# Projections from f16 parts, and row maxima combined between the turns of the next iteration

## Chip, cores and metric

One core of a Trainium2 chip. The time is that of the whole kernel on the device, in microseconds; the median of three runs before the change is 1688.91 (1688.57 to 1694.19).

## What is computed

A pre-norm block over x of shape (4, 2048, 256): causal attention with 16 heads of 16, then a product with int8-rounded operands.

```python
x = x + attn(layernorm(x), Wq, Wk, Wv, Wo, bo)
#   q, k, v = x @ Wq, x @ Wk, x @ Wv, split in 16 heads of 16
#   weights = softmax(q k^T / 4, causal); out = (weights v) @ Wo + bo
x = x + ffn(layernorm(x), rhs)
#   rows of the left operand and columns of rhs are scaled by their absolute maximum / 127,
#   rounded to integers, multiplied, scaled back
```

## The kernel before

There are two blocks of code. `project` goes over 16 chunks of 512 tokens. A chunk is normalised (statistics on VectorE, from chunk 2 on the normalisation itself on GpSimd, L595), transposed on TensorE in f32 (L773), copied to `xnT` by ScalarE (L732), and multiplied with the three weights in f32: four blocks of q and k (L792, j = 0 to 3, two products of 512 columns each), then two groups of v (L803, eight products of 256 columns each). The transposes of chunk n + 1 stand between q, k and v of chunk n. ScalarE casts each q or k block to f16 (L743), VectorE takes the rest as a second f16 part (L650), and both parts go to HBM. GpSimd also fills constants in K and V at the start.

`attend` goes over 16 iterations (4 batches by 4 groups of 4 heads). An iteration has 36 steps (`STEPS`, from the last query chunk to the first), each of two pairs of heads: TensorE makes scores (L1025), ScalarE takes exp (L1214), GpSimd masks the diagonal steps (L1277), TensorE multiplies with V three steps later (L1044). The scores need the row maximum subtracted, and that is inside the product: the negated maxima stand as two f16 rows in Q. They are found one iteration ahead by 68 "turns": TensorE makes a pair of banks of scores (`max_turn_on_pe`, L261 off the diagonal, L275 and L280 on it), VectorE reduces them (`max_turn_on_dve`, L353). Two pairs of banks alternate, so turn n needs turn n - 2 taken (`mx_free`). The 69th turn of an iteration is the tail: `combine_maxima` on VectorE (L308 to L316) makes negm and its two f16 parts, TensorE transposes them (L291), VectorE copies them to mT (`take_maxima`, L326), and SP writes four row transfers to Q (`max_rows`, L224), for which the scores of the next iteration's first step wait.

Every engine's queue is in the order of the program. On TensorE the order in `attend` is a table by hand, `BEFORE`: for each of the 72 pairs of an iteration how many turns come ahead of the value blocks, how many value blocks, how many turns behind them; then come the pair's scores. In pairs 58 to 62 it reads (2, 0, 0), (0, 2, 0), (0, 2, 0), (0, 1, 1), (2, 0, 0): two turns, then four value blocks with no turn, a fifth, the tail, and two turns of the next iteration. The turns of the first iteration are spread over chunks 2 to 13 of the projections, six places a chunk, behind each j and about v; its tail is in chunk 14, and the first 12 turns of the next iteration are in chunks 14 and 15. A last phase (output projection, second normalisation, integer product) runs under the last iteration and behind it.

## Time and profile before

| | us |
|---|---|
| median of the runs | 1688.91 |
| span of the profiled execution | 1686.8 |
| around the span (the difference of these) | 2.1 |
| attention block begins on TensorE | 249.6 |
| last turn's reduce ends, all engines | about 1455 |
| TensorE busy | 1603.7 |
| VectorE busy | 1516.0 |
| ScalarE busy | 1330.8 |
| GpSimd busy | 290.6 |

The busy time of TensorE counts the modelled drain of each matmul, so a busy TensorE isn't one without gaps. A group's mean is the length of one instruction with its start and drain; instructions of one engine overlap by some 0.07 to 0.2 us, so the pace is read from starts. "Idle before" is time of an engine just before an instruction, with what ended it; "issue" means nothing that the profile shows.

### The profile page before, as it was taken

What the parts mean: (1) busy time and instruction counts of PE and PEld (TensorE: products, weight loads), DVE (VectorE), ACT (ScalarE), POOL (GpSimd) and SP (SyncE); (2) the same over time, 40 slices, a digit from 0 to 9 for tenths busy, and PEclk for the clock granted to TensorE, in tenths of its full rate; (3) what the DMA queues carried; (4) which work ended last, traced back from release to release, by engine and by line L of the source; (5) the groups of instructions that cost most, each with busy time, mean ns of one, the idle gap of its engine ahead of it and who ended that gap; (6) DMA issues with size and microseconds to landing.
All of it is one profiled execution on the core that took longest, in us unless ns stands there. A gap on an engine that the chain in (4) does not pass through costs nothing.

```text
span 1686.8 us, 39739 instructions
## 1 busy us (share of the span) xinstructions
PE 1603.7 (95%) x16319; PEld 643.5 (38%) x16319; DVE 1516.0 (90%) x1812; ACT 1330.8 (79%) x2610; POOL 290.6 (17%) x363
## 2 busy tenths in 40 slices
PE   6999999999999999999999999999999999999965
PEld 3445443333333333333333333333333333344433
DVE  4677779999999999999999999999999999678876
ACT  2233338999999999999999999999999999877651
POOL 5333310201020202111111111111112020100120
PEclk9999999999999999999999999999999999999986
DMA  3443320111121212121212112121212143034532
GB/s 108 146 136 117 112 89 12 39 34 40 33 77 37 74 38 68 43 62 43 62 47 59 54 52 59 46 60 46 59 46 67 47 115 88 14 105 136 159 116 70
DMA packets 105609, 118.73 MB, mean 70 GB/s; under 512 B 20688, under 2 KB 87508, under 8 KB 105428
## 3 DMA queue, kind: packets, MB, share of 16 engines
q1 hardware_dynamic: 105428, 116.19, 23.8%
q8 instruction: 129, 2.11, 0.5%
...
## 4 chain that ended last, share of the span: by engine, by line
DVE 54%; PE 27%; issue 1%; ACT 1%; DMA 1%; SPq 1%; POOL 0%; ACTq 0%; DVEq 0%
DVE pmax L353 46%; PE psum L1044 11%; PE psum L1025 6%; DVE pblk L353 4%; PE psum L1084 3%; PE psum L261 3%; PE psum L280 2%; PE psum L275 2%; DMA f_rs<-inverse_sums 1%; DVE V L1323 1%; ACT prob L1214 1%; PE psum L1108 1%; DVE V L1342 1%; DVE V L1330 1%; DVE f_amax L1348 1%
## 5 line engine op out<-in xcount | busy, mean ns | idle before, releaser
L1214 ACT ACTIVATE prob<-psum 128x512 f32<-128x512 f32 (+1 forms) x2304 | 1181.0, 574 | 136.7 <-PE psum L1025 113.2
L353 DVE TENSOR_REDUCE pmax<-psum 128x2 f32<-128x1024 f32 (+1 forms) x960 | 1101.0, 1216 | 13.5 <-PE psum L280 6.5
L1044 PE MATMUL psum<-prob,V 128*32 128x256 f32 x8704 | 676.0, 391 | 0.0
L1025 PE MATMUL psum<-Q,K 50*128 50x512 f16 (+3 forms) x2560 | 464.7, 349 | 3.8 <-ACT prob L1214 1.0
L1277 POOL TENSOR_SCALAR_AFFINE_SELECT prob<-prob 128x512 f32<-128x512 f32 x256 | 160.6, 640 | 1185.3 <-ACT prob L1214 1182.8
L261 PE MATMUL psum<-K,Q 48*128 48x512 f16 x1536 | 298.4, 385 | 13.5 <-DVE pmax L353 13.5
L1044 PEld LDWEIGHTS psum<-prob,V 128*32 128x32 f32 x8704 | 181.5, 108 | 294.2 <-issue 214.1
L1025 PEld LDWEIGHTS psum<-Q,K 50*128 50x128 f16 x2560 | 174.6, 94 | 251.3 <-ACT prob L1214 185.1
L261 PEld LDWEIGHTS psum<-K,Q 48*128 48x128 f16 x1536 | 74.3, 93 | 272.0 <-DVE pmax L353 212.8
L353 DVE TENSOR_REDUCE pblk<-psum 128x8 f32<-128x1024 f32 x128 | 151.8, 1219 | 5.8 <-PE psum L280 5.6
L280 PE MATMUL psum<-K,Q 48*128 48x512 f16 (+3 forms) x1024 | 128.6, 298 | 0.0
L275 PE MATMUL psum<-mask,maskid 64*128 64x128 bf16 (+2 forms) x1280 | 103.6, 230 | 9.3 <-DVE pmax L353 5.3
L743 ACT CAST part<-psum 128x512 f16<-128x512 f32 x64 | 37.5, 586 | 91.8 <-PE psum L792 91.8
L650 DVE TENSOR_TENSOR part<-psum,part 128x512 f16<-128x512 f32 x64 | 44.3, 692 | 60.5 <-ACT part L743 60.5
L595 POOL TENSOR_SCALAR f_x<-f_x,mv,rstd 128x256 f32<-128x256 f32 x56 | 67.7, 1223 | 117.2 <-DVE rstd L635 116.9
L275 PEld LDWEIGHTS psum<-mask,maskid 64*128 64x128 bf16 x1280 | 58.4, 95 | 62.9 <-DVE pmax L353 35.1
L1084 PE MATMUL psum<-f_wo,f_us 128*128 128x256 f32 x256 | 76.5, 429 | 0.0
L803 PE MATMUL psum<-wv,xnT 128*128 128x256 f32 x256 | 63.1, 390 | 0.0
L792 PE MATMUL psum<-xnT,wq 128*128 128x512 f32 x128 | 62.0, 617 | 1.1 <-DVE wq L688 1.1
L792 PE MATMUL psum<-xnT,wk 128*128 128x512 f32 x128 | 62.5, 614 | 0.0
L753 ACT COPY V<-psum 128x512 f32<-128x512 f32 x32 | 18.8, 586 | 46.1 <-PE psum L803 46.1
L1084 PEld LDWEIGHTS psum<-f_wo,f_us 128*128 128x128 f32 x256 | 47.5, 204 | 18.0 <-issue 12.6
...
## 6 DMA issues: line engine op xcount, KB each, us to landing
...
Q<-q_parts SPq DMA_DIRECT2D x128, 64.0 KB, 2.5
K<-k_parts SPq DMA_DIRECT2D x128, 64.0 KB, 2.1
...
```

The source lines that it names most:

```text
L261: return nc.tensor.matmul(bank, Q[p][rows, pair, qt * P:(qt + 1) * P], K[p][rows, pair, kc * CH:(kc + 1) * CH], start=True, stop=True)
L275: nc.tensor.matmul(to, maskid[at:at + HALF, i, :], mk, start=i == 0, stop=False, skip_group_check=True)
L280: m = nc.tensor.matmul(bank[:, col:col + n], Q[p][rows, pair, qt * P:(qt + 1) * P], K[p][rows, pair, a * CH:a * CH + n], start=False, stop ...
L353: nc.vector.tensor_reduce(to, of, axis=AX.X, op=ALU.max).then_inc(M.mx_free, 1)
L595: i = nc.gpsimd.tensor_scalar(xn[s][:, t, :], xs[s][:, t, :], mv[s][:, t, 0:1], rstd[s][:, t:t + 1], ALU.subtract, ALU.mult)
L792: m = nc.tensor.matmul(PS[:, j, :], w[i][:, k, o * P:(o + 1) * P], xnT[s][:, k, :], start=k == 0, stop=k == KC - 1)
L803: m = nc.tensor.matmul(PS[:, 2 + j, (t % 2) * D:(t % 2 + 1) * D], xnT[s][:, k, t * P:(t + 1) * P], w[2][:, k, :], start=k == 0, stop=k == ...
L1025: m = nc.tensor.matmul(PS[:, SB + i % RING, at:at + n], K[it % 2][rows, pair, kb * P:(kb + 1) * P], Q[it % 2][rows, pair, (c + 1) * CH - n ...
L1044: m = nc.tensor.matmul(PS[32 * h:32 * h + 32, UB, to:to + n], V[:, it // NG * NT + kb, col:col + 32], prob[(it * NSTEP + k) % PRING][:, h, ...
L1084: m = nc.tensor.matmul(bank[:, q % 2 * D:(q % 2 + 1) * D], us[j % 4][:, o, q * P:(q + 1) * P], wo[:, o, :], start=False, stop=o == KC - 1, ...
L1214: nc.scalar.activation(prob[g % PRING][:, h, 0:n], PS[:, SB + i % RING, 0:n], ACT.Exp, scale=by).then_inc(exp_done, 1)
L1277: nc.gpsimd.affine_select(out=d, in_=d, compare_op=ALU.is_ge, fill=0.0, base=0, pattern=[[0, G], [1, P]], channel_multiplier=-1).then_inc( ...
```

## The change

The parts of the projection: x and the weights are each split into two f16 parts, high and low, and three of the four products of parts are added in PSUM (`TERMS`), so a f32 product becomes three f16 ones. The q and k weights are scaled by a power of two and split on VectorE; the v weight is transposed, scaled by powers of two for each output column, split, and transposed back, and Wo is scaled by the inverse in `attend` on GpSimd (two operations of 128x256 in iteration 1). x is normalised in halves, ScalarE casts each half (`high_rows`), GpSimd subtracts (`low_rows`), TensorE transposes both parts in f16, ScalarE copies both. `root(1)` now stands ahead of `take_xT(0)`.

The parts of the maxima: pmax and pblk exist twice, by the parity of the iteration. The tail of iteration it - 1 is no longer right behind its last turn but between the fifth and the sixth turn of iteration it (`BETWEEN`). VectorE does the blocks behind the first of these turns and negm behind the second; GpSimd does the split into parts; ScalarE copies the transposed parts to mT. A tail gives nothing to `mx_free`; the turn two behind it waits for `mT_ready`. The first iteration's tail stays whole in chunk 14, and the last one's is at the end. `BEFORE` and `AHEAD` are as they were.

```diff
...
+TERMS = ((0, 0), (1, 0), (0, 1))
...
-    turns, tail = [], []
+    turns, tail, last = [], [], []
     for it in range(ITS):
-        turns += [(it, kind) for kind in (KINDS if it else sorted(KINDS, key=lambda kind: max(chunks_of(kind))))]
-        tail.append(len(turns))
-        turns.append((it, None))
-    return turns, tail
-
-
-TURNS, TAIL = order_of_turns()
+        kinds = KINDS if it else sorted(KINDS, key=lambda kind: max(chunks_of(kind)))
+        for i, kind in enumerate(kinds):
+            if it >= 2 and i == BETWEEN:
+                tail.append(len(turns))
+                turns.append((it - 1, None))
+            turns.append((it, kind))
+        last.append(len(turns) - 1)
+        if it in (0, ITS - 1):
+            tail.append(len(turns))
+            turns.append((it, None))
+    return turns, tail, last
+
+
+BETWEEN = 5
+TURNS, TAIL, LAST = order_of_turns()
+
+
+def handed_back(n):
+    return sum(kind is not None or it == 0 for it, kind in TURNS[:n])
 
...
+def pairs_of_turns():
+
+    out, turn = {}, BEGUN
+    for it in range(ITS):
+        for pair in range(2 * NSTEP):
+            back = turns_until(it, pair)[1]
+            for n in range(turn, back):
+                out[n] = (it, pair)
+            turn = max(turn, back)
+    return out
+
+
+PAIR_OF = pairs_of_turns()
+TAKEN_AT = {PAIR_OF[TAIL[it]]: it for it in range(1, ITS)}
+PARTS_AT = {PAIR_OF[min(LAST[it] + 2, TAIL[it])]: it for it in range(1, ITS)}
...
-        pe.wait_ge(mx_free, n - 1)
+        pe.wait_ge(mx_free, handed_back(n - 1))
+        if TURNS[n - 2][1] is None and TURNS[n - 2][0] >= 1:
+            pe.wait_ge(M.mT_ready, TURNS[n - 2][0] + 1)
     at = MB + 2 * (n % 2)
...
+def blocks_to_maxima(nc, dve, it, M):
+
+    dve.wait_ge(M.mx_free, handed_back(LAST[it] + 1))
+    blk = M.pblk[it % 2][:].rearrange("p f h a j -> p (f h a) j")
+    top = M.pmax[it % 2][:].rearrange("p f h (a t) j -> p (f h a) t j", t=TPC)
     nc.vector.tensor_reduce(top[:, :, 2, 3], blk[:, :, 0:3], axis=AX.X, op=ALU.max)
-    nc.vector.tensor_copy(top[:, :, 0, 3], blk[:, :, 3]).then_inc(comb, 1)
-    dve.wait_ge(comb, it * COMB + 1)
-    nc.vector.tensor_reduce(negm[:], pmax[:].rearrange("p f h q j -> p (f h q) j"), axis=AX.X, op=ALU.max,
-                            negate=True).then_inc(comb, 1)
-    dve.wait_ge(comb, it * COMB + 2)
-    nc.vector.tensor_scalar(mparts[:, 0, :], negm[:], 1.0 / ONE, None, ALU.mult).then_inc(comb, 1)
-    dve.wait_ge(comb, it * COMB + 3)
+    nc.vector.tensor_copy(top[:, :, 0, 3], blk[:, :, 3]).then_inc(M.blocks_in, 1)
+
+
+def negated_maxima(nc, dve, it, M):
+
+    dve.wait_ge(M.blocks_in, it + 1)
+    if it >= 1:
+        dve.wait_ge(M.mp_ready, it)
+    nc.vector.tensor_reduce(M.negm[:], M.pmax[it % 2][:].rearrange("p f h q j -> p (f h q) j"), axis=AX.X, op=ALU.max,
+                            negate=True).then_inc(M.negm_ready, 1)
+
+
+def split_maxima(nc, dve, M):
+
+    negm, mparts = M.negm, M.mparts
+    dve.wait_ge(M.negm_ready, 1)
+    nc.vector.tensor_scalar(mparts[:, 0, :], negm[:], 1.0 / ONE, None, ALU.mult).then_inc(M.first_part, 1)
+    dve.wait_ge(M.first_part, 1)
     nc.vector.scalar_tensor_tensor(out=mparts[:, 1, :], in0=negm[:], scalar=1.0 / ONE, in1=mparts[:, 0, :],
                                    op0=ALU.mult, op1=ALU.subtract).then_inc(M.mp_ready, 1)
 
 
+def split_maxima_on_pool(nc, pool, it, M):
+
+    negm, mparts, scaled = M.negm, M.mparts, M.scaled
+    pool.wait_ge(M.negm_ready, it + 1)
+    pool.wait_ge(M.mT_ready, it)
+    nc.gpsimd.tensor_scalar(scaled[:], negm[:], 1.0 / ONE, 1.0, ALU.mult, ALU.mult).then_inc(M.first_part, 1)
+    pool.wait_ge(M.first_part, 3 * it - 1)
+    nc.gpsimd.tensor_copy(mparts[:, 0, :], scaled[:]).then_inc(M.first_part, 1)
+    pool.wait_ge(M.first_part, 3 * it)
+    nc.gpsimd.tensor_tensor(mparts[:, 1, :], scaled[:], mparts[:, 0, :], ALU.subtract).then_inc(M.first_part, 1)
+    pool.wait_ge(M.first_part, 3 * it + 1)
+    pool.sem_inc(M.mp_ready, 1)
+
...
+def take_maxima_on_act(nc, act, it, PS, M):
+
+    n = TAIL[it]
+    act.wait_ge(M.mrows_in, it * M.MROWS)
+    act.wait_ge(M.mx_ready, n + 1)
+    nc.scalar.copy(M.mT[:], PS[:, M.MB + 2 * (n % 2), :].bitcast(F16)[:, 0:P]).then_inc(M.mT_ready, 1)
+
+
...
-                pool.wait_ge(xn_ready, n)
-                pool.wait_ge(tposed, n - 1)
+                pool.wait_ge(xn_ready, 2 * n)
+                pool.wait_ge(xl_ready, 2 * n - 2)
                 for t in range(TPC):
-                    i = nc.gpsimd.tensor_scalar(xn[s][:, t, :], xs[s][:, t, :], mv[s][:, t, 0:1],
-                                                rstd[s][:, t:t + 1], ALU.subtract, ALU.mult)
-                i.then_inc(xn_ready, 1)
-
-
-            pool.wait_ge(w_scaled, 2)
-            pool.wait_ge(xn_ready, 2)
+                    i = nc.gpsimd.tensor_scalar(xn[s][:, t, :], xs[s][:, t, :], nmean[s][:, t:t + 1],
+                                                rstd[s][:, t:t + 1], ALU.add, ALU.mult)
+                    if t % 2 == 1:
+                        i.then_inc(xn_ready, 1)
+
+            def low_rows(n):
+                s = n % 2
+                for half in range(2):
+                    at = slice(2 * half, 2 * half + 2)
+                    pool.wait_ge(xh_ready, 2 * n + half + 1)
+                    if n >= 2 and half == 0:
+                        pool.wait_ge(tposed, n - 1)
+                    nc.gpsimd.tensor_tensor(xp[s][:, 1, at, :], xn[s][:, at, :], xp[s][:, 0, at, :],
+                                            ALU.subtract).then_inc(xl_ready, 1)
+
...
+            low_rows(2)
...
+            def scale_value_weight():
+
...
+                dve.wait_ge(vT_raw, 1)
+                of = PS[:, 6, :].rearrange("p (o r) -> p o r", o=KC)
+                nc.vector.tensor_reduce(cmax[:], of, axis=AX.X, op=ALU.max,
...
+                dve.wait_ge(v_step, 5)
+                for o in range(KC):
+                    nc.vector.tensor_scalar(vT[:, 0, o, :], of[:, o, :], cinv[:, o:o + 1], None,
+                                            ALU.mult).then_inc(v_step, 1)
+                dve.wait_ge(v_step, 5 + KC)
+                for o in range(KC):
+                    i = nc.vector.scalar_tensor_tensor(out=vT[:, 1, o, :], in0=of[:, o, :], scalar=cinv[:, o:o + 1],
+                                                       in1=vT[:, 0, o, :], op0=ALU.mult, op1=ALU.subtract)
+                i.then_inc(vT_split, 1)
 
             statistics(0)
             variance(0)
-            nc.vector.memset(M.pmax[:], NEG).then_inc(pmax_set, 1)
+            for s in range(2):
...
+            def high_rows(n, half):
+                s, at = n % 2, slice(2 * half, 2 * half + 2)
+                act.wait_ge(xn_ready, 2 * n + half + 1)
+                if n >= 2 and half == 0:
+                    act.wait_ge(tposed, n - 1)
+                nc.scalar.copy(xp[s][:, 0, at, :], xn[s][:, at, :]).then_inc(xh_ready, 1)
+
             def take_xT(n):
                 act.wait_ge(tposed, n + 1)
                 if n >= 2:
                     act.wait_ge(v_ready, (n - 1) * KC)
-                nc.scalar.copy(xnT[n % 2][:], PS[:, 0:2, :]).then_inc(xT_ready, 1)
+                for i in range(2):
+                    nc.scalar.copy(xT[n % 2][:, i].rearrange("p k t -> p (k t)"),
+                                   PS[:, i, :].bitcast(F16)).then_inc(xT_ready, 1)
 
             root(0)
+            for half in range(2):
+                high_rows(0, half)
+            root(1)
             take_xT(0)
-            root(1)
+            for half in range(2):
+                high_rows(1, half)
+            act.wait_ge(vT_back, 1)
+            nc.scalar.copy(wp[2][:].rearrange("p i k c -> p (i k c)"),
+                           PS[:, 7, :].bitcast(F16)).then_inc(wv_ready, 1)
             for n in range(NC):
                 s = n % 2
                 for j in range(QK):
                     if n >= 2 and j == 0:
                         act.wait_ge(stored[s], n // 2 * STORES)
                     nc.scalar.copy(part[s][0][:, j], PS[:, j, :]).then_inc(hi_ready, 1)
+                    if j % 2 == 1 and 2 <= n + 1 < NC:
+                        high_rows(n + 1, j // 2)
                 if n + 1 < NC:
                     take_xT(n + 1)
...
             def transpose(n):
                 s = n % 2
-                pe.wait_ge(xn_ready, n + 1)
+                pe.wait_ge(xl_ready, 2 * n + 2)
                 if n >= 1:
                     pe.wait_ge(lo_ready, (n - 1) * QK + 2)
-                for f in range(KC):
-                    for t in range(TPC):
-                        i = nc.tensor.transpose(PS[:, f, t * P:(t + 1) * P], xn[s][:, t, f * P:(f + 1) * P],
-                                                identf[:])
-                i.then_inc(tposed, 1)
-
-            transpose(0)
+                for i in range(2):
+                    for f in range(KC):
+                        for t in range(TPC):
+                            at = (f * TPC + t) * P
...
+                        for o in range(KC):
+                            at = ((i * KC + k) * KC + o) * P
+                            m = nc.tensor.transpose(PS[:, 7, :].bitcast(F16)[:, at:at + P],
+                                                    vT[:, i, o, k * P:(k + 1) * P], identh[:])
+                m.then_inc(vT_back, 1)
+
             pe.wait_ge(wmax_ready, 1)
             nc.tensor.transpose(PS[0:2, 7, 0:P], wmax[:], identf[:]).then_inc(wmaxT, 1)
+            value_weight(False)
+            transpose(0)
...
             nc.tensor.matmul(PS[:, 7, 256:258], ones2[:], gdiag[:], start=True, stop=True).then_inc(pow_spread, 1)
             for n in range(NC):
                 s = n % 2
-                pe.wait_ge(xT_ready, n + 1)
+                pe.wait_ge(xT_ready, 2 * n + 1)
...
-                        pe.wait_ge(w_scaled, i + 1)
+                        pe.wait_ge(w_scaled, 2 * i + 2)
                     if n >= 1 and i == 1:
                         pe.wait_ge(v_taken, (n - 1) * KC + o + 1)
-                    for k in range(KC):
-                        m = nc.tensor.matmul(PS[:, j, :], w[i][:, k, o * P:(o + 1) * P], xnT[s][:, k, :],
-                                             start=k == 0, stop=k == KC - 1)
+                    for of_w, of_x in TERMS:
+                        if j == 0 and of_x == 1:
+                            pe.wait_ge(xT_ready, 2 * n + 2)
+                        for k in range(KC):
+                            m = nc.tensor.matmul(PS[:, j, :], wp[i][:, of_w, k, o * P:(o + 1) * P],
+                                                 xT[s][:, of_x, k, :], start=(of_w, of_x, k) == (0, 0, 0),
+                                                 stop=(of_x, k) == (1, KC - 1))
                     m.then_inc(qk_ready, 1)
+                    if n == 0 and j == 1:
+                        value_weight(True)
                     turns(n, j)
...
                             act.wait_ge(p_free, g - PRING + 1)
                         nc.scalar.activation(prob[g % PRING][:, h, 0:n], PS[:, SB + i % RING, 0:n],
                                              ACT.Exp, scale=by).then_inc(exp_done, 1)
+                        if h % 2 == 1 and (it, 2 * k + h // 2) in TAKEN_AT:
+                            take_maxima_on_act(nc, act, TAKEN_AT[it, 2 * k + h // 2], PS, M)
                         if h % 2 == 1 and it + 1 == ITS:
                             for p, u in units_at(2 * k + h // 2):
                                 unit(p, u)
...
                     if k == ENDS[1] + 1 and 2 <= it < WHOLE + 2:
                         normalise_group(it - 2)
+                    for pair in (2 * k, 2 * k + 1):
+                        if (it, pair) in PARTS_AT:
+                            split_maxima_on_pool(nc, pool, PARTS_AT[it, pair], M)
...
-                if it >= 2 and n == (TAIL[it] + TAIL[it - 1]) // 2:
+                if it >= 2 and n == (LAST[it] + LAST[it - 1]) // 2:
                     invert(it - 2)
-                max_turn_on_dve(nc, dve, n, PS, M)
+                if TURNS[n][1] is not None:
+                    max_turn_on_dve(nc, dve, n, PS, M)
+                if it >= 2 and n == LAST[it - 1] + 1:
+                    blocks_to_maxima(nc, dve, it - 1, M)
+                if it >= 2 and n == LAST[it - 1] + 2:
+                    negated_maxima(nc, dve, it - 1, M)
+            blocks_to_maxima(nc, dve, ITS - 1, M)
+            negated_maxima(nc, dve, ITS - 1, M)
```

## Rows read from the trace of the kernel before

**Rows 1.** The page, part 4: chain that ended last, share of the span by line.
```profile
DVE pmax L353 46%; PE psum L1044 11%; PE psum L1025 6%; DVE pblk L353 4%; PE psum L1084 3%; PE psum L261 3%; PE psum L280 2%; PE psum L275 2%; DMA f_rs<-inverse_sums 1%; DVE V L1323 1%; ACT prob L1214 1%; PE psum L1108 1%; DVE V L1342 1%; DVE V L1330 1%; DVE f_amax L1348 1%
```
**Rows 2.** VectorE in order of time, iteration 4: start us, us, operation, count, idle before.
```profile
602.81 0.54 DVE L1289 RECIPROCAL f_inv<-f_sums 128x64 f32<-128x64 f32 x1
...
610.51 30.63 DVE L353 TENSOR_REDUCE pmax<-psum 128x2 f32<-128x1024 f32 x27
...
641.13 2.36 DVE L353 TENSOR_REDUCE pblk<-psum 128x8 f32<-128x1024 f32 x2
...
643.53 0.20 DVE L308 TENSOR_REDUCE pmax<-pblk 128x16 f32<-128x48 f32 x1
...
643.85 0.42 DVE L311 TENSOR_REDUCE negm<-pmax 128x64 f32<-128x256 f32 x1
...
645.47 0.23 DVE L326 COPY mT<-psum 128x128 f16<-128x128 f16 x1 [0.71 <-PE psum L291]
...
646.05 3.72 DVE L353 TENSOR_REDUCE pmax<-psum 128x2 f32<-128x1024 f32 x3 [0.35 <-PE psum L280]
...
683.91 0.54 DVE L1289 RECIPROCAL f_inv<-f_sums 128x64 f32<-128x64 f32 x1
```
**Rows 3.** TensorE (PE matmul, PEld weight load) in order of time, same place.
```profile
641.19 0.12 PEld L275 LDWEIGHTS psum<-mask,maskid 64*128 64x128 bf16 x4 [0.39 <-DVE pmax L353]
...
645.13 0.10 PEld L291 LDWEIGHTS psum<-identh,mparts 128*128 128x128 f16 x1 [0.41 <-issue]
...
645.39 0.26 PEld L275 LDWEIGHTS psum<-mask,maskid 64*128 64x128 bf16 x4
...
651.18 0.39 PE L261 MATMUL psum<-K,Q 48*128 48x512 f16 x2
```
**Rows 4.** Projection stage in order of time: first chunk, chunk 2, a steady chunk, chunk 14.
```profile
17.90 5.63 PE L792 MATMUL psum<-xnT,wq 128*128 128x512 f32 x8 [1.07 <-DVE wq L688]
...
19.50 0.38 DVE L630 BATCH_NORM_AGGREGATE mv<-stats 128x2 f32<-128x6 f32 x4
...
54.72 1.41 DVE L623 BATCH_NORM_STATS2 stats<-f_x 128x6 f32<-128x256 f32 x4 [2.79 <-DMA f_x<-in_L_attn_x]
...
59.64 1.88 PE L792 MATMUL psum<-xnT,wq 128*128 128x512 f32 x4
...
107.78 0.39 PE L261 MATMUL psum<-K,Q 48*128 48x512 f16 x2
...
108.10 1.98 PE L792 MATMUL psum<-xnT,wk 128*128 128x512 f32 x4
...
110.01 0.39 PE L261 MATMUL psum<-K,Q 48*128 48x512 f16 x2
...
116.48 1.99 PE L803 MATMUL psum<-wv,xnT 128*128 128x256 f32 x8
...
219.74 3.60 PE L792 MATMUL psum<-xnT,wq 128*128 128x512 f32 x8
```
**Rows 5.** A bf16 product of the last phase; two groups by line (busy, mean ns).
```profile
1507.79 1.05 PE L1108 MATMUL psum<-f_wq,V 128*128 128x256 bf16 x8
...
L743 ACT CAST part<-psum 128x512 f16<-128x512 f32 x64 | 37.5, 586 | 91.8 <-PE psum L792 91.8
...
L1247 POOL TENSOR_TENSOR f_rs<-f_rs 128x1024 f32<-128x1024 f32 x12 | 28.4, 2367 | 9.3 <-DMA f_rs<-inverse_sums 9.2
```
**Rows 6.** SP's transfers of the maxima, their landing, and the scores that need them.
```profile
645.78 2.50 SPq L224 DMA_DIRECT2D Q<-mT  x4
...
DMA to landing us min/median/max: 1.8/1.9/3.2
...
656.89 0.38 PE L1025 MATMUL psum<-Q,K 50*128 50x512 f16 x2
```
**Rows 7.** Windows: span, busy (count) by engine PE to POOL, PEclk, DMA share, GB/s.
```profile
54.50:57.50 3.00, 0.23 (x6) 0.19 (x7) 2.78 (x10) 0.59 (x1) 0.00 (x0) 1.00 0.54 185
...
254.00:258.00 4.00, 3.98 (x34) 1.86 (x30) 3.83 (x4) 2.65 (x7) 0.00 (x0) 0.50 0.01 4
```

141 lines of the change are left out of this document (99 added, 42 removed).

## The prediction

> **What bounds the kernel now.** I read the chain of waits by line first [rows 1]: VectorE's row-maximum reduces (pmax and pblk, L353) are half of it, the rest mostly TensorE. Then VectorE in order of time over one period of the attention stage [rows 2]. The same reciprocal comes at 602.81 and 683.91, so an iteration takes 81.10 us. Twenty-seven reduces take 30.63, thus (30.63 - 1.22) / 26 = 1.131 us each when they follow each other, and 68 of them are 76.9; the reciprocal is about 0.5; from the natural end of the second pblk (641.13 + 2 x 1.13 = 643.40) to the next turn (646.05) go 2.65. Sum 80.05; about 1.0 is small idle time. VectorE has no slack: what is taken from it or made idle counts one to one, unless TensorE can't follow. Then TensorE around that place [rows 3]: it issues the last turn of the iteration's maxima at 641.19 and reaches the transposition of the maxima at 645.13 without waiting for VectorE (its idle time there is "issue"). In between it does scores and five value blocks. So VectorE's combining sits beside 3.94 us in which TensorE has no turn to give it. That is what decides this part.
> The projection stage [rows 4] is different: from chunk 3 (59.64) to chunk 14 (219.74) a chunk takes 160.1 / 11 = 14.55 us, and TensorE's products follow each other. It is bound by TensorE there.
>
> **Projections, steady chunks.** Now: a q or k block of two f32 products is 110.01 - 108.10 = 1.91 us, its turn 108.10 - 107.78 = 0.32. No row shows f16 products of 128 rows and 512 columns; the nearest are eight bf16 ones of 256 columns in 1.05, 0.21 of it the drain, so about 0.107 each [rows 5]. Six of 512 columns are then 1.28, with the change of weights some 1.35: 0.55 saved, four times, 2.2 a chunk. A value group (eight f32, 1.99 with 0.2 of drain) becomes twelve of 0.107: 1.3, so 0.5 saved twice, 1.0. Transposes: f16, twice as many, taken as equal. TensorE thus saves 3.2. Against this there is a new chain before the transposes of the next chunk. The second `high_rows` stands on ScalarE behind the cast of j = 3, and the second `low_rows` on GpSimd behind that, while TensorE waits in order for xl_ready with V, the turns and the next chunk queued behind. After the last k product: cast 0.6 [rows 5], high part of 128x512 0.7 (a cast from SBUF, estimated a little over the cast from PSUM), low part 1.2 (half of GpSimd's 128x1024 two-input operation, 2.37) [rows 5], 0.1 of semaphores: 2.6; only the turn (0.32) covers it. Stall 2.3. Before, xn was long ready. The two xT copies (1.0 each instead of one) lie beside V, the normalisation on GpSimd lies before, and VectorE's work of about 11 a chunk stays under 13.4. Net 0.9 to 1.15 a chunk; I take 1.15, since the blocks of turns also shrink: 11 x 1.15 = 12.7. Bounds: if the low part took half or twice as long, the net is 1.75 or 0, so 19 or 0. Chunk 14 brings 0.9, and chunk 15, which has no next transposes, 2.1 before VectorE's eight turns bind.
> **Its start.** `root(1)` now stands ahead of `take_xT(0)`, so the first product, at 17.90 now, waits for a variance that ends at 19.88 now, and later still behind two more weight operations; then VectorE's split of the value weight and TensorE's transposes of it stand ahead of k of chunk 0, all of it behind ScalarE and GpSimd, whose 7 us fills of K follow. I estimate chunk 1 three us late, chunk 2 four. But at 54.72 VectorE idles 2.79 for x [rows 4], and a stall of the same kind stands before the chunk before; both vanish in the delay. Left at chunk 3: +1.3 (bounds 0 and +5).
> Projection stage: +1.3 - 12.7 - 0.9 - 2.1 = -14.4, bounds -24 and +3.
>
> **Combining, taken apart, iteration by iteration.** VectorE loses the two splits, the wait for TensorE's transposition (0.71 [rows 2]) and the copy to mT; it keeps blocks (643.53 to 643.85, 0.32) and negm (0.42). On paper 2.65 - 0.74 = 1.9 saved. But the table BEFORE, which places turns among scores and values, is unchanged: two value blocks, twice, and no turn between LAST and the 70th place. So the first turn of the next iteration takes the place of the old transposition, at 645.13. From the weight load of such a diagonal turn to VectorE's start go 646.05 - 645.39 = 0.66: it starts at 645.79, and VectorE idles from 643.40 until then, 2.4 us, because blocks_to_maxima is written behind that turn and not in the hole. Then: turn 645.79 to 646.92, blocks to 647.24, turn to 648.37, negm to 648.83, three turns to 652.2. The old end of the same five turns is 652.00. So far +0.2.
> TensorE must be checked along: the third turn needs the first one done (646.92; before, the short mT copy freed that bank at 645.7), so TensorE stands 1.2 longer there, with scores and values queued behind it, and runs about 1.1 late to the fifth turn; that is just in time for VectorE.
> Then comes the transposition, now between the fifth and the sixth turn, and it takes one of the two banks. TensorE may issue the sixth turn only when VectorE is through with the fifth, at 652.2, instead of at 651.18 ahead of need [rows 3]. A turn of this kind takes about 0.45 from issue to VectorE's start (0.39 of it the product): after the 0.2 for issuing, VectorE starts at 652.87 instead of 652.00. That makes +0.87, and another 0.15 follow, since TensorE, 1.2 late, has less lead for the two turns after it. An iteration thus gets 1.0 longer instead of 1.9 shorter. Bounds: if TensorE's values slid forward into the gaps, 0; if each of the bubbles is half as large again, +2.2; the paper value -1.9 is the far end. 14 iterations have this order (the tails of 1 to 14): 14 x 1.0 = +14, bounds -27 and +31.
> Beside it: the split on GpSimd is three operations of 64 columns; by 2.37 for 1024 columns 0.15 each, with starts and semaphores 0.7 to 1.2 in all. It starts at 648.9 and TensorE comes for it at about 651: hidden, with a second to spare, and the masking of the same step comes after it in time for values three steps later. The copy on ScalarE costs some 0.2 a period there, and ScalarE had idle time. It stands behind the exponentials of its pair of heads, so mT is ready at 653.3 and not at 645.7. SP then issues four transfers (2.50) and they land 1.9 after issue [rows 6]: about 657.2. The first scores that need them stood at 656.89; they are 1.0 later, 657.9. Hidden, by 0.7. What else SP has to store or load at that time waits for later steps anyway. The last tail has no turn behind it and frees nothing that anyone waits for: 0. Scaling Wo on GpSimd, the second copies of pmax and pblk: 0.
>
> **The sum.** The profiled execution has a span of 1686.8; the runs' median is 1688.91, 2.1 more for what lies around the span. 1686.8 - 14.4 + 14 = 1686.4; with 2.1, 1688.5.
>
> **Rivals.**
> (a) *The combining gain comes through.* TensorE's stretch at 641.19 to 645.13 would have to shrink, or VectorE to catch up elsewhere. For it: VectorE is the first line of the chain. Against it: the stretch in [rows 3] has no wait in it that could go. -27 - 14: 1688.9 - 41 = 1648. Chance 0.12; half-way cases 0.05.
> (b) *The chain behind the cast costs less* (GpSimd's low part at half the price, or the start hidden): projections -24, combining +14: 1679. With combining at +7: 1672. For it: the 1.2 is from f32 in and out. Chance 0.18.
> (c) *The row maxima come too late.* Place: scores of the next iteration, step 0. From 0.7 us more than I count (a landing took up to 3.2 [rows 6], against 1.9), TensorE stops there, and each us beyond, less the 0.4 of lead that VectorE has, lengthens 14 iterations. At 1.7 more: 14 x 0.9 = +13, so 1702, slower than before. Chance 0.15. Slower without this, by bubbles of twice the size or a dearer start: 1698 to 1710, chance 0.05.
> (d) *TensorE's clock falls in the new stalls.* It stood at 0.50 (1.2 GHz) in 254 to 258, after TensorE had worked little at the change of stages, but at 1.00 (2.4 GHz) through the wait of 54.5 to 57.5 [rows 7], which is longer than my 2.3. If it fell in each of 12 chunks for those 4 us, TensorE would lose 2 us of work each time: +24, 1713. Chance 0.07.
> The Trainium skill, "TensorE: Matmul & The Clock Gate", Part 4 (PE-mode transpose), says that transposes don't count as activity for the clock gate; by it, stall and transposes together, about 3.3 us, are one quiet stretch. The rows show no such stretch in this stage, so this stays the small chance just given.
> (e) Forecast as summed: 0.38, its own range 1680.5 to 1697.
>
> **How the numbers follow.** Within 0.5% (8.4 us, about what a measurement can tell from no change): (e), 0.38. Faster: (a) 0.17 and (b) 0.18, 0.35. Slower: (c) 0.20 and (d) 0.07, 0.27. Range for 8 in 10: from between (b) and (a), 1664, to between (c) and (d), 1710. The time is that of (e), 1688.5.
>
> **What would show it.** Right: VectorE idle 2.2 to 2.6 once an iteration ahead of the first diagonal turn, released by TensorE, then 0.5 ahead of the sixth turn; period near 82.1; chunks of 13.4 with 2.3 of TensorE waiting for GpSimd ahead of the transposes; attention beginning about 14 earlier than at 249.6. Wrong: a period under 81, or of 83 and more with TensorE waiting for a DMA at the first scores; chunks under 12.5 or over 14; a clock of 0.50 inside the projections.

## The result, and the profile after

| | before | after |
|---|---|---|
| median of the runs, us | 1689.88 (1688.57 to 1694.19, 4 runs) | 1705.09 (1700.72 to 1706.28, 4 runs) |
| span of the profiled execution | 1686.8 | 1704.5 |
| attention begins on TensorE | 249.62 | 250.04 |
| one iteration of attention | 81.10 | 81.92 |

The changed kernel takes 1.0079 of the time before (95% interval 1.0064 to 1.0094): slower by 13 us by this ratio (by 15 by the two medians), where I had forecast no change. The ledger of the two profiled executions, by VectorE's reciprocals, one an iteration: the first stands level (359.51 and 359.44); thirteen periods of +0.82 are 10.7 (1413.84 and 1424.47); the one behind them, with the last maxima, takes 75.03 instead of 73.50, +1.5; so 12.2 at the end of attention, and the 5.5 that are left of 17.7 arise in the last phase. There the additions of VectorE keep a distance of 12.16 to those of before for ten tiles (1476.97 and 1489.13 the first, 1577.36 and 1589.52 the tenth) and then drift off, in a stretch in which the granted clock was 0.84 before and 0.81 after. From the last of these reciprocals to the end it takes 199.5 before and 205.0 here, and between 199.5 and 204.5 in the other kernels of this document, whose edits leave that phase alone. So I count no step of the change for it.

The projection stage of after, against [rows 4]: the first products of q in chunks 0, 3 and 14, one turn of the stall, the x that VectorE waits for, and SP's load of it.
```profile
24.22 4.90 PE L959 MATMUL psum<-f_rs,wpq 128*128 128x512 f16 x12 [5.91 <-ACT f_rs L865]
...
69.68 1.46 PE L959 MATMUL psum<-f_rs,wpq 128*128 128x512 f16 x6
...
98.66 2.75 PE L959 MATMUL psum<-f_rs,wpq 128*128 128x512 f16 x12
...
107.38 1.07 PE L918 MATMUL psum<-identh,f_us 128*128 128x128 f16 x16 [2.01 <-POOL f_us L684]
...
221.04 2.75 PE L959 MATMUL psum<-f_rs,wpq 128*128 128x512 f16 x12
```
```profile
50.57 1.41 DVE L713 BATCH_NORM_STATS2 stats<-f_x 128x6 f32<-128x256 f32 x4 [6.67 <-DMA f_x<-in_L_attn_x]
...
63.82 1.41 DVE L713 BATCH_NORM_STATS2 stats<-f_x 128x6 f32<-128x256 f32 x4 [5.37 <-DMA f_x<-in_L_attn_x]
```
```profile
46.51 0.42 SPq L628 DMA_DIRECT2D f_x<-in_L_attn_x  x1
...
59.89 0.43 SPq L628 DMA_DIRECT2D f_x<-in_L_attn_x  x1
```
Against 17.90, 59.64 and 219.74 of before, chunk 0 starts 6.3 later, chunk 3 10.0 later and chunk 14 1.3 later. The stall for GpSimd is there, 2.01. The wait for x, 2.79 before, did not vanish in the delay: it has grown to 5.37, and the one a chunk earlier from 2.14 to 6.67. SP issued the load that the later one waits for at 50.87 before and at 59.89 here. In 59 to 74 the granted clock is 0.77 here and 1.00 before, so a part of the 10.0 may be a slower TensorE; no run takes that part by itself.

The change of iterations in after, VectorE and then TensorE, against [rows 2, 3] (start, busy, operation, count, idle before):
```profile
645.87 1.21 DVE L416 TENSOR_REDUCE pblk<-psum 128x8 f32<-128x1024 f32 x1
649.26 1.23 DVE L416 TENSOR_REDUCE pmax<-psum 128x2 f32<-128x1024 f32 x1 [2.18 <-PE psum L315]
650.40 0.19 DVE L344 TENSOR_REDUCE pmax<-pblk 128x16 f32<-128x48 f32 x1
650.51 0.17 DVE L345 COPY pmax<-pblk 128x16 f32<-128x16 f32 x1
650.59 1.22 DVE L416 TENSOR_REDUCE pmax<-psum 128x2 f32<-128x1024 f32 x1
651.73 0.41 DVE L353 TENSOR_REDUCE negm<-pmax 128x64 f32<-128x256 f32 x1
...
656.19 5.92 DVE L416 TENSOR_REDUCE pmax<-psum 128x2 f32<-128x1024 f32 x5 [0.66 <-PE psum L296]
```
```profile
650.54 0.35 PE L310 MATMUL psum<-mask,maskid 64*128 64x256 bf16 x4 [0.81 <-DVE pmax L416]
...
654.53 0.23 PE L328 MATMUL psum<-identh,mparts 128*128 128x128 f16 x1
...
655.76 0.39 PE L296 MATMUL psum<-K,Q 48*128 48x512 f16 x2
```
VectorE's chain has become shorter, and TensorE's turns don't come sooner: it idles 2.18 ahead of the first diagonal turn and 0.66 ahead of the sixth.

### The profile page after: what moved, and what is told of

Read it like the earlier page. It is cut to its first block, busy times and chain, and to the rows that moved or that the text cites. A ratio compares the mean times of both kernels' runs of the same rounds, so it can differ in the third digit from the quotient of the medians.

```text
span 1704.5 us, 40744 instructions
## 1 busy us (share of the span) xinstructions
PE 1575.4 (92%) x16715; PEld 625.7 (37%) x16715; DVE 1514.0 (89%) x1795; ACT 1365.3 (80%) x2674; POOL 302.7 (18%) x442
## 3 DMA queue, kind: packets, MB, share of 16 engines
q8 instruction: 132, 2.16, 0.6%
## 4 chain that ended last, share of the span: by engine, by line
DVE 49%; PE 34%; issue 1%; ACT 1%; DMA 0%; SPq 0%; POOL 0%; ACTq 0%; DVEq 0%; POOLq 0%
DVE pmax L416 42%; PE psum L1220 14%; PE psum L1201 7%; PE psum L296 3%; PE psum L1261 3%; PE psum L310 2%; DVE pblk L416 2%; PE psum L315 2%; DVE V L1528 1%; DVE V L1509 1%; DVE V L1516 1%; DVE f_amax L1534 1%; ACT prob L1392 1%; PE psum L1285 1%; PE psum L1274 0%
## 5 line engine op out<-in xcount | busy, mean ns | idle before, releaser
L296 PEld LDWEIGHTS psum<-K,Q 48*128 48x128 f16 x1536 | 74.2, 93 | 253.9 <-DVE pmax L416 193.7
L865 ACT COPY f_rs<-psum 128x1024 f16<-128x1024 f16 x32 | 30.8, 1014 | 36.1 <-PE psum L918 36.1
L959 PE MATMUL psum<-f_rs,wpq 128*128 128x512 f16 x192 | 47.8, 393 | 5.9 <-ACT f_rs L865 5.9
L976 PE MATMUL psum<-wpv,f_rs 128*128 128x256 f16 x384 | 53.1, 295 | 0.0
L684 POOL TENSOR_TENSOR f_us<-f_x,f_us 128x512 f16<-128x512 f32 x32 | 36.9, 1155 | 80.0 <-ACT f_us L858 80.0
L315 PEld LDWEIGHTS psum<-K,Q 48*128 48x128 f16 x1024 | 48.1, 96 | 0.6
```

The source lines that it names most:

```text
L296: return nc.tensor.matmul(bank, Q[p][rows, pair, qt * P:(qt + 1) * P], K[p][rows, pair, kc * CH:(kc + 1) * CH], start=True, stop=True)
L315: m = nc.tensor.matmul(bank[:, col:col + n], Q[p][rows, pair, qt * P:(qt + 1) * P], K[p][rows, pair, a * CH:a * CH + n], start=False, stop ...
L959: m = nc.tensor.matmul(PS[:, j, :], wp[i][:, of_w, k, o * P:(o + 1) * P], xT[s][:, of_x, k, :], start=(of_w, of_x, k) == (0, 0, 0), stop=( ...
L976: m = nc.tensor.matmul(PS[:, 2 + j, (t % 2) * D:(t % 2 + 1) * D], xT[s][:, of_x, k, t * P:(t + 1) * P], wp[2][:, of_w, k, :], start=(of_w, ...
```

## The experiments

Each kernel ran on the same chip as runs of the kernel before; ratios are to those. Where no ratio is given, the kernel ran once. The starts of attention are of one profiled execution each: four kernels with the projections of after unchanged (after, projections only, blocks in the hole, shifted table) give 249.47 to 252.15, so a difference of 2 or 3 us in that number alone is no finding.

**Each half of the change alone.** The first has the new projections and the old combining, the second the old projections and the new combining.

> The new projections with the old maxima. Theory (from the two traces): the attention block begins where it did (249.6 against 250.0), because a start 10 us later (chunk 3 at 69.7, not 59.6) eats what the chunks save; an iteration keeps its 81.1. So 1690, ratio 1.000, plus up to 6 where the clock falls longer in the last phase. Rival: the new projections are what costs (parts, more clock drops, more GpSimd work), attention begins late too: 1696 or more.

> The old projections with the new maxima. Theory: attention begins at 249.6, an iteration takes 81.92 instead of 81.10, 14 of them 11.5 more: 1701.4, ratio 1.007. Rival: the longer iteration comes from the projections' side effects (buffers, the clock): then 81.1 and ratio 1.000.

Projections only: 1691.16 (1688.63 to 1699.76), ratio 1.001 (0.9991 to 1.0029); attention at 249.74, period 81.08. Maxima only: 1704.28 (1701.7 to 1705.21), ratio 1.0085 (1.006 to 1.0111); attention at 248.88, period 81.92. So the loss of 13 to 14 is all of the combining, about as summed (+14) and 2.9 above what I expected of this kernel, where I had left out the 1.5 behind the last maxima; and the projections bring nothing where I had summed 14.4. The two are independent.

**Blocks and negm ahead of the first diagonal turn**, in VectorE's hole:
```diff
-                if TURNS[n][1] is not None:
-                    max_turn_on_dve(nc, dve, n, PS, M)
                 ... (blocks_to_maxima, negated_maxima at this place)
+                if TURNS[n][1] is not None:
+                    max_turn_on_dve(nc, dve, n, PS, M)
```


> The changed kernel, but VectorE does blocks and negm ahead of the first turn of the next iteration, where it is idle 2.2 us. Theory: 0.74 of VectorE's work goes into idle time, 14 x 0.74 = 10 us less than the changed kernel, period 81.2, time about 1695. Rival: TensorE's lateness behind the hole sets the pace, not VectorE's work: then period 81.7 to 81.9 and no change (1703 to 1705).

1705.7, ratio 1.0091 (1.0065 to 1.0117), period 81.92 to the hundredth. VectorE around the change of iterations in this kernel:
```profile
650.43 0.21 DVE L344 TENSOR_REDUCE pmax<-pblk 128x16 f32<-128x48 f32 x1
650.55 0.18 DVE L345 COPY pmax<-pblk 128x16 f32<-128x16 f32 x1
650.76 0.42 DVE L353 TENSOR_REDUCE negm<-pmax 128x64 f32<-128x256 f32 x1
652.57 3.49 DVE L416 TENSOR_REDUCE pmax<-psum 128x2 f32<-128x1024 f32 x3 [1.39 <-PE psum L315]
656.42 2.41 DVE L416 TENSOR_REDUCE pblk<-psum 128x8 f32<-128x1024 f32 x2 [0.36 <-PE psum L315]
659.50 2.36 DVE L416 TENSOR_REDUCE pmax<-psum 128x2 f32<-128x1024 f32 x2 [0.66 <-PE psum L296]
```
The three operations lie in the hole now, 0.74 less on VectorE's path, and nothing is gained by it: the sixth turn starts 6.93 behind the first one in both kernels (656.19 - 649.26 and 659.50 - 652.57), now with 0.36 of waiting for TensorE between the third and the fourth besides the 0.66. The rival was right: here TensorE's order sets the pace.

**A shifted table of turns**, on top of that kernel: rows 58 to 62 of `BEFORE`.
```diff
-    ... (2, 0, 0), (0, 2, 0), (0, 2, 0), (0, 1, 1), (2, 0, 0), ...
+    ... (2, 0, 0), (0, 1, 1), (0, 2, 0), (0, 2, 1), (1, 0, 0), ...
```


> The changed kernel with the two blocks of the maxima built ahead of the first diagonal turn (as in the kernel of the blocks in the hole, whose period stayed at 81.92) and, besides, TensorE's turn table shifted so that its diagonal turns have less between the first and the third (rows 58 to 62 of the table). Theory (TensorE's own order sets the 0.82 us more of each iteration: it stands at the reduction of the maxima before it may go on with work that was ready): the period falls by 0.3 to 0.9, to 81.0 to 81.6. Rival (VectorE's chain ahead of the third turn is what is long, and TensorE's order is filled around it): the period stays at 81.9 or gets longer, since the moved matmuls now come late somewhere else.

Period 81.39, so 0.53 of the 0.82 came back; one run, 1701.64, its span 1699.9, 4.6 below after's 1704.5 and still above the kernel before. VectorE there:
```profile
646.83 2.36 DVE L416 TENSOR_REDUCE pmax<-psum 128x2 f32<-128x1024 f32 x2 [0.56 <-PE psum L315]
649.85 2.41 DVE L416 TENSOR_REDUCE pblk<-psum 128x8 f32<-128x1024 f32 x2 [0.66 <-PE psum L315]
652.92 9.31 DVE L416 TENSOR_REDUCE pmax<-psum 128x2 f32<-128x1024 f32 x8 [0.67 <-PE psum L296]
```
What is left are three waits of 0.6 for single turns of TensorE. With TensorE's order changed and VectorE's as it was, the period moved; with VectorE's alone it did not. No run moves the tail from its place between the fifth and the sixth turn, so what that place costs by itself is summed and not shown.

**High parts earlier.** ScalarE makes the high parts of the next chunk behind the casts of j = 0 and 1 instead of 1 and 3.
```diff
-                    if j % 2 == 1 and 2 <= n + 1 < NC:
-                        high_rows(n + 1, j // 2)
+                    if j < 2 and 2 <= n + 1 < NC:
+                        high_rows(n + 1, j)
```


> The changed kernel, but ScalarE makes the high parts of the next chunk behind the casts of j = 0 and 1, not of 1 and 3, so GpSimd's low parts are done before TensorE comes to the transposes. Theory: the 2.0 to 2.4 us in which TensorE waits for GpSimd in each chunk go: chunks of 11.5 to 12 instead of 13.5, attention begins 15 to 20 us earlier, 1686. Rival: the chunk is bound elsewhere (VectorE's 11 us, the loads of x), so only 5 us come back: 1700.

1685.61 (1682.64 to 1688.35), ratio 0.9972 (0.9959 to 0.9985), though the slower combining is still in it; attention at 231.85, 18.2 earlier than in after. A steady chunk in it, on TensorE:
```profile
175.43 1.07 PE L918 MATMUL psum<-identh,f_us 128*128 128x128 f16 x16
...
179.02 0.39 PE L296 MATMUL psum<-K,Q 48*128 48x512 f16 x2 [0.79 <-DVE pmax L416]
...
187.55 1.07 PE L918 MATMUL psum<-identh,f_us 128*128 128x128 f16 x16
```
The chunk takes 12.12 and the wait for GpSimd is gone; a wait of 0.79 for VectorE comes next. Both numbers are as I expected. The granted clock over 74 to 224 is 1.00. Chunk 2's transposes come 2.5 earlier (42.48), but chunk 3's first product stands at 69.63, where it was, for VectorE still waits for x there. One line of order on ScalarE was worth more than the rest of the change.

**Dummy products in the stall**, issued just ahead of TensorE's wait for the low parts; eight of 128x128, results unused.
```diff
+                if n >= 2:
+                    for i in range(8):
+                        nc.tensor.matmul(PS[:, i % 2, :], wp[0][:, 0, 0, 0:P], xT[(n - 1) % 2][:, 0, 0, :], ...)
                 pe.wait_ge(xl_ready, 2 * n + 2)
```


> The changed kernel with eight dummy products of 128x128 issued by TensorE in front of its wait for the low parts in chunks 2 to 15, into banks that are free there; their results are never read. Theory of the clock (the stall of 2 us for GpSimd in each chunk, with the transpositions around it, is what makes the granted clock fall in some chunks; that is why the steady chunk saves 0.74 and not 1.15): the low-clock stretches between 59 and 230 go, steady chunks are 13.4 to 13.5 without the longer ones, and attention begins 2 to 5 us ahead of 250.04. Rival (the clock's dips there are of the transpositions, or the dummies push the real ones out): the dips stay or the chunk gets longer than 13.6, and attention begins at 249 to 253.

Attention at 246.56, 3.5 earlier (time 1698.77), with the same chain for GpSimd (TensorE, two chunks):
```profile
185.70 1.90 PE L915 MATMUL psum<-f_rs,wpq 128*128 128x512 f16 x8
187.88 1.07 PE L922 MATMUL psum<-identh,f_us 128*128 128x128 f16 x16 [0.28 <-POOL f_us L684]
...
201.32 0.90 PE L922 MATMUL psum<-identh,f_us 128*128 128x128 f16 x13 [0.27 <-POOL f_us L684]
```
The windows of after and then of this kernel (span, busy and count by engine PE to POOL, granted clock, DMA share, GB/s):
```profile
79.00:83.00 4.00, 3.89 (x33) 2.75 (x34) 2.98 (x8) 1.93 (x2) 0.05 (x1) 0.60 0.51 168
...
74.00:224.00 150.00, 127.29 (x896) 66.84 (x895) 118.47 (x218) 71.88 (x121) 49.33 (x66) 0.98 0.43 130
```
```profile
74.00:224.00 150.00, 147.41 (x1002) 74.11 (x1002) 121.16 (x224) 74.23 (x124) 50.02 (x67) 1.00 0.43 130
```
In after the granted clock was at 1.00 (2.4 GHz) before 79 and fell to 1.2 GHz for most of 79 to 83, behind a stall of 1.93 and the transposes that end it; the mean of 74 to 224 is 0.98. With products in the stall it is 1.00 throughout, though the dummies hold TensorE busy and the useful work waits just as long. From the transposes of chunk 4 to those of chunk 15 a chunk is 13.63 in after ((229.07 - 79.11) / 11) and 13.35 here ((227.16 - 80.31) / 11). The clock thus cost 3 us in this stretch. (The same eleven chunks take 146.85 here, 149.96 in after and 148.4 to 151.4 in three other kernels with these projections, so 1.5 to 4.6.) It is my case (d), at an eighth of its price. By the Trainium skill ("TensorE: Matmul & The Clock Gate", Part 4: PE-mode transpose) transposes do not count as TensorE being busy in the same way. These traces fit that and do not single it out: with the transposes kept and only the stall gone, in the kernel of the early high parts, the clock stays at 1.00 as well, and in the kernel with the addition (below) it fell behind a wait with no f16 transposes near it.

**SP loads x ahead.** The load for chunk n + 3 right behind the stores of k of chunk n, ahead of the loads for attention.
```diff
-                if n + 2 < NC:
-                    sp.wait_ge(xn_ready, 2 * n + 2)
-                    load(n + 2)
+                if n == 0:
+                    sp.wait_ge(xn_ready, 2)
+                    load(2)
                 ... (stores of q and k)
+                if n + 3 < NC:
+                    sp.wait_ge(xn_ready, 2 * n + 4)
+                    load(n + 3)
```


> The changed kernel with SP issuing the load of chunk n+3's x behind the k stores of chunk n, ahead of the stores of v and the loads for attention; nothing else. Theory (VectorE's idle 6.67 us at 50.57 and 5.37 us at 63.82 are for x tiles whose load stood behind other issues on SP): both waits fall under 1 us, chunk 3's transpositions begin at 59 to 62 instead of 69.68, and attention begins 6 to 10 us ahead of 250.04, near 240 to 244. Rival (VectorE would be late for chunk 3 in any case, for its evictions follow TensorE's products, which began late): the waits turn into waits for TensorE, chunk 3 comes at most 2 us earlier and attention stays within 2 us of 250.

(The 69.68 that the expectation calls transpositions is chunk 3's first product of q.) That product is at 64.94, 4.7 earlier; the waits of 6.67 and 5.37 for x are gone, but for 0.36 ahead of the statistics at 43.98; attention is at 246.70, 3.3 earlier, and the one time is 1698.94. Both lie between theory (59 to 62 for the product, attention 6 to 10 earlier) and rival, so the theory promised about twice of what came. What follows the wait for x is VectorE's wait for ScalarE's root and TensorE's for GpSimd (1.93). In the kernel of both, early high parts and early loads (below), the product is at 60.94, only 1.3 behind the 59.64 of before, though chunk 1 is as late as in after. So another 4.0 of the 10.0 hangs on the place of the high parts, which brings nothing at chunk 3 as long as VectorE waits for x.
```profile
57.53 1.40 DVE L716 BATCH_NORM_STATS2 stats<-f_x 128x6 f32<-128x256 f32 x4
...
64.04 0.17 DVE L728 TENSOR_SCALAR nmean<-mv 128x4 f32<-128x4 f32 x1 [1.30 <-ACT std L854]
...
73.20 1.39 DVE L716 BATCH_NORM_STATS2 stats<-f_x 128x6 f32<-128x256 f32 x4
```

**Four orders of the start.** First, `take_xT(0)` back ahead of `root(1)` on ScalarE:

> The changed kernel with one line moved: ScalarE copies the two halves of chunk 0's transposed x ahead of its second square root instead of behind it. Theory (the 10.1 us by which chunk 3 starts late begin with the first product, 24.22 against 17.90, which waits 5.91 us for ScalarE behind the square root of 22.97): the first product of chunk 0 stands near 18 to 20, the transpositions of chunk 1 some 2 to 4 us ahead of 33.70, and half or more of this is left at chunk 3 (69.68), so attention begins 1 to 4 us ahead of 250.04. Rival (what starts chunks 2 and 3 is the load of x behind SP's other issues alone): the first product is early, but chunk 3 keeps 69 to 70 and attention its 250.

Both were wrong. The first product came at 20.12, and chunk 1's transposes at 37.53 instead of 33.70; attention at 258.36, the one time 1710.5. VectorE and GpSimd in it:
```profile
26.29 1.07 DVE L799 TENSOR_SCALAR v_cmax<-v_cmax 128x2 int32<-128x2 int32 x1
27.40 3.53 DVE L802 TENSOR_SCALAR f_vback<-v_cmax 128x2 f32<-128x2 f32 x1
30.96 0.17 DVE L804 RECIPROCAL v_cinv<-f_vback 128x2 f32<-128x2 f32 x1
```
```profile
27.40 7.06 POOL L664 MEMSET K<- 32x4096 f16 x2
```
An operation on 128x2 numbers took 3.53 us: it starts with the first of GpSimd's two fills and ends with it (7.06 / 2). The reciprocal of 128x2 behind it took its 0.17 beside the second fill. The scaling of the value weight hangs on it, and behind that k of chunk 0. Then the fills of K at GpSimd's very start, alone and with this order of ScalarE:

> The changed kernel with GpSimd filling the constant rows of K (two fills, 7.07 us at 28.03) at its very start, where it idles from 5.2 to 13.6, instead of behind the low parts of chunk 1. Theory (in the changed kernel the fills, 10 us with those of V, push GpSimd's normalisation and low parts of chunk 2, so that the transpositions of chunk 2 wait for GpSimd at 44.98, and chunk 3 follows): GpSimd's normalisation of chunk 2 starts at 37.4 when the root is there, the transpositions of chunk 2 move by 0 to 2 us, the loads behind them the same, and attention begins 0 to 3 us ahead of 250.04. The theory that the fills are most of the late start would want 5 us or more.

> The kernel with the fills first and, besides, ScalarE's copies of the transposed x of chunk 0 ahead of its second square root. With the square root alone moved, the first product came at 20.12 instead of 24.22, yet chunk 1 came 3.8 us later: a VectorE operation of 128x2 (27.40, L802) took 3.53 us, from the start of a GpSimd fill of 3.53 us. Theory (that fill held it): with the fills at the start this operation takes about 1.0 or less, the value weight is split by 30, k of chunk 0 starts near 30 and chunk 1 at 33.0 to 34.2, so 3.5 to 4.5 ahead of the 37.53 of that kernel. Rival (the operation was slow for another reason, such as ScalarE or a PSUM bank): it takes 2.5 or more again and chunk 1 stays at 37 or later.

Alone: transposes of chunk 1 at 34.39 and of chunk 2 at 45.67, later by 0.7, attention at 256.25, 6.2 later where I expected 0 to 3 earlier, the one time 1710.03. The fills were not what made chunk 2 late (the early high parts had brought it to 42.48), and early fills made VectorE late at its first normalisation. Together with ScalarE's order: chunk 1 at 37.65, no gain, because the fills of V took the place of those of K; attention at 255.24, the one time 1709.08.
```profile
28.15 2.73 DVE L802 TENSOR_SCALAR f_vback<-v_cmax 128x2 f32<-128x2 f32 x1
```
```profile
28.15 0.96 POOL L692 MEMSET V<- 128x1024 f32 x1
29.04 1.82 POOL L693 MEMSET V<- 128x1024 f32 x1
```
The same operation starts at 28.15 with them and ends at 30.88, as they do (29.04 + 1.82 = 30.86). My expected number failed and the rival's came; but what the rows show is not the rival's reason (ScalarE or a PSUM bank): this small operation is held until a fill of GpSimd ends (there the first of the two, here the second). The Trainium skill ("SBUF — State Buffer", Who interferes with whom) has the two engines share a pair of ports as an exclusive lock, which in VectorE's two-port modes the first to issue holds for its whole instruction. These rows fit it; no row tells the mode. Other VectorE operations beside the fills of after (the statistics, 1.40 for four; operations with an operand in PSUM, 0.88 for two) kept their lengths.

The fourth order takes the value weight out of GpSimd's way: VectorE scales and splits it ahead of chunk 1's statistics, and ScalarE's two copies stand ahead of the second root. It is built on the best kernel below.
```diff
+            scale_value_weight()
             statistics(1)
             ...
             normalise(1)
-            scale_value_weight()
```


> The kernel of early high parts, early x loads and old maxima (1666.6 us, attention at 225.47) with the start in another order: VectorE scales and splits the value weight ahead of chunk 1's statistics, and ScalarE does the copies of chunk 0's transposed x and of the value weight ahead of its second square root. Theory (of the late start, 6.9 us by chunk 1 against the kernel before, a part is the order: the first product behind the square root, and the value weight's scaling on VectorE beside GpSimd's operations, where two tiny ones took 1.00 and 1.08): the first product comes at 20.1 instead of 24.2, the tiny operations take 0.15 to 0.3, chunk 1's transpositions stand at 31 to 32.5 instead of 33.61, and attention begins 1 to 3 us earlier; the time is 1663.5 to 1666. Rival (the root of chunk 1, now later, delays chunk 1's low parts and all that follows): chunk 1 at 33.5 or later, attention at 225 to 229, 1666 to 1670.

```profile
20.06 4.27 PE L898 MATMUL psum<-f_rs,wpq 128*128 128x512 f16 x12 [1.85 <-DVE wpq L725]
...
30.76 1.86 PE L857 MATMUL psum<-identh,f_us 128*128 128x128 f16 x16 [3.17 <-DVE part L684]
...
44.98 1.89 PE L857 MATMUL psum<-identh,f_us 128*128 128x128 f16 x16 [4.10 <-POOL f_us L626]
...
223.35 0.59 PE L1140 MATMUL psum<-Q,K 50*128 50x512 f16 x3 [0.93 <-PEq L484]
```
```profile
22.14 0.17 DVE L742 TENSOR_SCALAR f_vback<-v_cmax 128x2 f32<-128x2 f32 x1
```
The small operations take 0.17 each, and chunk 1 stands at 30.76, 2.9 earlier: a part of its lateness was order. But chunk 2 stands at 44.98 against 42.48 (TensorE waits 4.10 for GpSimd, whose fills now run 30.57 to 40.4, ahead of its normalisation of chunk 2), and chunk 3's first product at 63.20 against 60.94, so nothing of it is left there. Attention begins at 223.35, 2.1 earlier, as expected, but not for that reason: the gain arises between the transposes of chunks 5 and 7 (82.56 to 106.82, against 80.70 to 108.92), where VectorE waits 1.59 and 2.19 for x in the kernel that this one is built on, and not at all here. Why x is in time here was not tested. The time is within the range expected: 1665.37 (1662.1 to 1667.21), ratio 0.9847 (0.9829 to 0.9866).

**Adding the negated mean, in the kernel before.**
```diff
-  nc.gpsimd.tensor_scalar(xn, xs, mv[s][:, t, 0:1], rstd[s][:, t:t + 1], ALU.subtract, ALU.mult)
+  nc.gpsimd.tensor_scalar(xn, xs, nmean[s][:, t:t + 1], rstd[s][:, t:t + 1], ALU.add, ALU.mult)
```


> The kernel before (old projections, old maxima) with one thing of the change: the mean is negated by VectorE, and GpSimd's normalisation of 128x256 adds it instead of subtracting the mean. In the changed kernel four of them take 2.17 us, in the kernel before 4.85. Theory (the operation pair costs it, add and multiply against subtract and multiply): four take 2.1 to 2.3 us here as well; attention still begins at 248.5 to 250.5, since TensorE sets the pace. Rival (it is the other surroundings, tile addresses or VectorE's traffic, that made it faster): they take 4.8 us here.

```profile
32.25 2.16 POOL L596 TENSOR_SCALAR f_x<-f_x,nmean,rstd 128x256 f32<-128x256 f32 x4 [0.21 <-POOL V L606]
```
Four take 2.16 instead of 4.85. Attention began at 251.53, outside of what I expected: the first block of q took 6.70 instead of 5.63, and in 57 to 62 the granted clock was 0.66 where it was 1.00 in the same window of before, though TensorE's wait ahead of it was the shorter one (1.86 against 2.77); why, I can't say, and this is one execution; the one time, 1691.55, is 0.1 above the highest of the seven runs of the kernel before beside it (1686.99 to 1691.45). So the operation got cheaper, and as expected that brought no time in a stage that TensorE bounds.

**What the parts are worth together.** High parts and x early, with the old combining and the old start:

> The new projections with the old combining of the maxima, with ScalarE's high parts behind the casts of j = 0 and 1, and SP's x load of chunk n+3 behind the k stores. Theory (the parts add: projections with early high parts put attention at 231.85, x loads 3.3 us earlier, period 81.1): attention begins at 226 to 230, the period is 81.1, and the time is 1668 to 1677, a ratio of 0.988 to 0.993 to the kernel before. Rival (with chunks of 12.0 the x loads come too late in every chunk, or they collide with stores): attention at 231 to 236, 1676 to 1684.

```profile
60.94 1.46 PE L898 MATMUL psum<-f_rs,wpq 128*128 128x512 f16 x6
```
1666.62 (1664.58 to 1669.58), ratio 0.9865 (0.9849 to 0.9882): faster than both kernels, and a little better than expected. Attention at 225.47, period 81.08; the line is chunk 3's first product of q. The gains at the start of attention add to more than their sum (18.2 and 3.3 alone, 24.3 against the 249.74 of projections only). The same projections with the new combining, blocks in the hole and the shifted table:

> The changed kernel with all that helped it: early high parts, early x loads, blocks of the maxima ahead of the first turn, and the shifted turn table (period 81.39 there). Theory (the parts are independent): attention begins at 224 to 227, the period is 81.35 to 81.45, against 81.08 with the old maxima, and the time is 14 x 0.31 = 4.3 us above the 1666.6 of the same projections with the old maxima: 1668 to 1673. Rival (in that table the new order costs nothing by itself): 1665 to 1667.

1678.64 (1673.49 to 1682.95), ratio 0.9923 (0.9894 to 0.9951); attention at 225.69, period 81.39. The period is as expected; the time is 12 above the kernel with the old combining, not 4.3. Of the 10.5 between the two profiled spans, thirteen periods of +0.31 give 4.0. The interval behind them, the one with the last maxima, takes 80.1 instead of 73.5, +6.6. TensorE there, and the window of that place (columns as above):
```profile
1434.04 0.64 PE L1223 MATMUL psum<-prob,V 128*32 128x256 f32 x8
1437.62 0.27 PE L328 MATMUL psum<-identh,mparts 128*128 128x128 f16 x1 [2.94 <-POOLq L378]
```
```profile
1436.00:1444.00 8.00, 6.12 (x42) 1.87 (x43) 0.40 (x1) 3.07 (x7) 0.78 (x3) 0.57 0.03 6
```
The last maxima have no turns behind them that would let TensorE go on, so it waits 2.94 for GpSimd's split, and behind that wait the clock is at 0.57. In the kernel of the shifted table alone the same wait is 2.94 and the interval 79.06; in after 0.29 and 75.03, with the clock at 1.00. A table that is better in the middle exposes the tail at the end. The rest of the 12 lies in the spread of the runs, 9.5 between the lowest and the highest of this kernel's four.

## Why the prediction was wrong

**The step that failed is the projections' start**: "Left at chunk 3: +1.3 (bounds 0 and +5)". It is +10.0. I had chunk 1 three us late and chunk 2 four; both are 7 late (33.70 against 26.80, 44.98 against 38.00). I saw that the first product would wait for the root and put no number of its own on the chain: variance, root, copy, and the value weight's scaling, in which two operations of 128x2 take 1.00 and 1.08 beside GpSimd. Then came the worse error. I counted VectorE's waits for x [rows 4] as slack in which 2 to 3 us of delay vanish. A wait absorbs a delay only if what it waits for does not move, and SP's load of x stands in order behind stores of q and k and loads for attention that come with the chunks. The load moved too, and the wait grew. Its issue moved by 9.0 (50.87 and 59.89). Putting the load ahead gave back 4.7 of the 10.0 at chunk 3. With the high parts early besides, 1.3 are left (60.94 against 59.64; 2.2 in the kernel with the new combining and the shifted table, 61.79): the stall for GpSimd, which I had counted in the steady chunks, stands ahead of chunks 2 and 3 too (2.43 and 1.93), and I had no term for it there. So the lateness of chunk 1, 6.9 in that kernel as well, does nearly vanish by chunk 3, as I had argued, once neither the load nor the high parts move with it. The reordered start gave back 2.9 of it at chunk 1, on another kernel, and nothing of that was left at chunk 3.

**The steady chunk**: 1.15 forecast, 0.79 measured ((221.04 - 69.68) / 11 = 13.76), 8.7 instead of 12.7. In a stretch with the clock at 1.00 it was right: 134.79 - 121.36 = 13.43, with 2.0 of waiting for GpSimd (2.3 forecast) and q or k blocks of six products in 1.47 with the drain. The difference is the clock, case (d), given 0.07: not in every chunk, but in some. Chunks 14 and 15 brought 0.9 instead of 3.0. There VectorE's turns bind from 241 on (three waits of TensorE for pmax, 0.49, 0.74 and 0.73; before two from 243, 0.74 and 0.22), and the granted clock is 0.93 in 224 to 248, against 1.00 before and 1.00 with the products in the stall. I had allowed for neither.

**The combining** was right in size and in mechanism: +0.82 an iteration for 1.0, idle 2.18 for 2.4 and 0.66 for 0.5, the hole filled by nothing, TensorE waiting 0.81 ahead of the third turn for the first one's reduce (1.2 forecast), the copy and SP's transfers hidden (the transposition at 654.53, SP at 656.38, the first scores not waiting). Of the 14 iterations that I counted, thirteen periods are of this kind; the last tail, put at 0, cost 1.5, since nothing covers the way over GpSimd there. 14 forecast, 14.4 measured alone (0.0085 x 1690), 12.2 of it in the attention stage of either profile (this kernel's and after's). Rival (a) is refuted by the kernel with the blocks in the hole: not even a shorter chain on VectorE reaches the time while TensorE keeps its order.

**The sum.** With +10.0 - 8.7 - 0.9 = +0.4 for the projections instead of -14.4, the same sum gives 1703.3 with the combining as forecast; 1705.09 was measured. The time lies in my range of 1664 to 1710, and in the branch that I put at 0.05: 1698 to 1710, "by bubbles of twice the size or a dearer start". It was the dearer start, and that half of the branch deserved far more. Rival (b), to which I gave 0.18, names the right lever from the wrong side: the low part costs 1.16 as I had it, and the chain could be taken off the path by its place.
